# Gathered attention: unread identity products before every tile, scatters and later gathers spread out

## The reference

```python
# L2 feed-forward: one expert of seven per token, and a shared one
sel, p = the expert with the highest sigmoid, and its probability
switched = sum over e of where(sel == e, p, 0) * swiglu(x, ew1[e], ew2[e], ew3[e])
x = x + 0.5 / total_weight * swiglu(x, sw1, sw2, sw3) + switched / total_weight

# L3 attention: x normalised is the query, the context is key and value
logits = jnp.einsum('bsd,btd->bst', q, k) / jnp.sqrt(d_k)
logits = jnp.where(mask == 0, NEG, logits)
attn = jax.nn.softmax(logits, axis=-1)
o = jnp.einsum('bst,btd->bsd', attn, v)
x = x + layernorm(o) * gamma + beta
```

## Time and profile before

| | us |
|---|---|
| median of 3 runs | 2151.9 |
| lowest, highest | 2150.73, 2154.13 |
| the profiled execution | 2150.0 |
| its span | 2148.3 |
| TensorE busy | 1907.1 (89%) |
| VectorE busy | 1628.0 (76%) |
| ScalarE busy | 1364.7 (64%) |
| GpSimd busy | 1104.0 (51%) |
| L3a's gathers, first and last start | 1636.1, 1722.5 |
| L3a's transpositions of xhat, first and last start | 1661.8, 1785.4 |

### The profile page before, as it was taken

How to read it: one execution, slowest core, us unless ns; L and a number is a source line. 1 busy time by engine, 2 the same in 40 slices (tenths; PEclk the granted TensorE clock), 3 DMA queues, 4 the chain that set the end, 5 groups by cost and what they waited for, 6 DMA issues and landing times. The chain is left out here.

```text
span 2148.3 us, 86799 instructions
## 1 busy us (share of the span) xinstructions
PE 1907.1 (89%) x32111; PEld 1451.7 (68%) x32111; DVE 1628.0 (76%) x3712; ACT 1364.7 (64%) x3729; POOL 1104.0 (51%) x1286
## 2 busy tenths in 40 slices
PE   5999987989999979999989995999993973799998
PEld 3777754767777758888867773887772431677776
DVE  6788877866777768888856667777664786699998
ACT  4677766655555545666645554667772753599997
POOL 5566632873333325555568882756775754233332
PEclk9999996999999989999999997999996555799999
DMA  5111111000000002000001110113442520000000
GB/s 123 46 47 48 48 40 39 21 6 18 14 14 15 14 27 87 1 0 0 0 21 35 35 30 16 47 61 110 139 142 76 145 70 22 2 17 15 15 15 21
DMA packets 174358, 87.98 MB, mean 41 GB/s; under 512 B 70892, under 2 KB 168840, under 8 KB 174216
## 3 DMA queue, kind: packets, MB, share of 16 engines
q1 hardware_dynamic: 163656, 63.36, 11.0%
q0 software_dynamic: 7296, 21.38, 3.4%
q10 hardware_dynamic: 3264, 1.38, 0.3%
HBM read 66.13 MB, written 19.93 MB: 40 GB/s over the span
## 5 line engine op out<-in xcount | busy, mean ns | idle before, releaser
L1494 POOL TENSOR_TENSOR L1f_hl<-L1f_h,L1f_hh 128x512 fp32r<-128x512 f32 x128 | 167.2, 1307 | 126.1 <-DVE L1f_hh L1506 125.8
L1455 ACT ACTIVATE L1f_h<-L1f_H,L1f_w_b 128x512 f32<-128x512 f32 x192 | 132.0, 688 | 104.9 <-PE L1f_H L925 98.0
L399 POOL TENSOR_TENSOR L1a_wide<-L1a_flat,head_of_row 128x512 f32<-128x512 f32 x64 | 66.6, 1040 | 200.6 <-ACT L1a_flat L597 158.3
L399 POOL TENSOR_TENSOR L3f_wide<-L3f_flat,head_of_row 128x512 f32<-128x512 f32 x64 | 66.7, 1042 | 189.9 <-PE L3f_S L469 167.6
L1506 DVE CAST L1f_hh<-L1f_h 128x512 fp32r<-128x512 f32 x192 | 127.8, 672 | 31.7 <-ACT L1f_h L1455 30.6
L625 DVE TENSOR_REDUCE L1a_mx<-L1a_S 128x16 f32<-128x1024 f32 x64 | 78.4, 1224 | 80.8 <-PE L1a_S L469 80.8
L1841 ACT ACTIVATE L2f_both_act<-L2f_both_A 128x512 f32<-128x512 f32 x114 | 68.2, 598 | 92.1 <-PE L2f_both_G L925 91.2
L1872 DVE TENSOR_TENSOR L2f_both_h<-L2f_both_G,L2f_both_act 128x512 f32<-128x512 f32 x114 | 78.2, 686 | 63.6 <-ACT L2f_both_act L1841 63.1
L399 POOL TENSOR_TENSOR L0a_wide<-L0a_flat,head_of_row 128x512 f32<-128x512 f32 x64 | 66.6, 1040 | 95.0 <-ACT L0a_xhat L610 90.1
L625 DVE TENSOR_REDUCE L0a_mx<-L0a_S 128x16 f32<-128x1024 f32 x64 | 78.3, 1224 | 31.1 <-PE L0a_S L469 31.0
L1778 POOL TENSOR_TENSOR L2f_both_hl<-L2f_both_h,L2f_both_hh 128x512 fp32r<-128x512 f32 x66 | 85.6, 1297 | 31.4 <-ACT L2f_both_hh L1846 26.6
(11 more groups left out here) (534 smaller groups left out, 6815.6 us busy)
## 6 DMA issues: line engine op xcount, KB each, us to landing
L0a_mask_raw<-mask SPq DMA_DIRECT2D x256, 32.0 KB, 1.8
sorted_x<-L1f_zero SPq DMA_DIRECT2D x4, 1408.0 KB, 12.3
L2f_both_xhat<-sorted_x SPq DMA_DIRECT2D x22, 256.0 KB, 3.9
sorted_y<-L2f_both_y_out SPq DMA_DIRECT2D x22, 256.0 KB, 3.9
L0a_ctxT<-ctx_T SPq DMA_DIRECT2D x64, 64.0 KB, 1.9
L1a_ctxT<-ctx_T SPq DMA_DIRECT2D x64, 64.0 KB
L1a_mask_raw<-mask SPq DMA_DIRECT2D x256, 0.1 KB
L2a_ctxT<-ctx_T SPq DMA_DIRECT2D x64, 64.0 KB
```

Source lines behind the costliest of these rows:

```text
L399: pool.tensor_tensor(wide[:, s], flat[:, s, :].rearrange("p (b n) -> p b n", b=B2).unsqueeze(2).broadcast_to([P, B2, 4, S]), c.head_of_row ...
L1455: act.activation(h[:, q % 3, :], psH[:, q % 2, :], ACT.Relu, bias=b1[:, q:q + 1]).then_inc(h_kept, 1)
L1494: pool.tensor_tensor(hl[:, q % 3, :], h[:, q % 3, :], hh[:, q % 3, :], ALU.subtract).then_inc(hl_pool, 1)
```

## The change

Three edits in two functions.

1. `swiglu`: GpSimd issues 8 scatters at once. The other 56 follow in the shared part, four to a group of tiles: two behind the first pair of products of group u, one behind the second, one behind the third, for u from 0 to 13.
2. `gather_attention`: the first 20 gathers (`FREE`) are issued before the loop. Gather t from 20 on stands at step t-10 (`AHEAD = 10`) and waits for the transposition of tile t-22 (`xT_done`).
3. `gather_attention`: ahead of each tile's transposition, and ahead of its wait for `xhat`, TensorE multiplies a bf16 identity of 128x128 with itself into an unused part of the same PSUM bank, 48 times for tile 0 (behind a wait for the statistics of the first eight tiles), 8 times for tiles 1 to 15, 4 times from tile 16 on. Nobody reads these products.

```diff
 def swiglu(c, name, sems, r, IP, E):
 
+    EARLY = 8
...
-            for t in range(NT):
+            def scatter(t):
                 pool.indirect_dma_start(r.sorted_x, bass.IndirectOffsetOnAxis(ap=r.place[:, t:t + 1], axis=0),
                                         r.xhat[:, t, :], None).then_inc(scattered, 16)
 
+            for t in range(EARLY):
+                scatter(t)
+
             def step(i, r_):
                 for q in range(IC):
+                    for u, s in shared_at(i, r_, 2):
+                        first = EARLY + u * GT + (0, 2, 3)[q]
+                        for t in range(first, min(first + (2, 1, 1)[q], NT)):
+                            wait(pool, a_done, u * IC + q + 1)
+                            scatter(t)
...
-    LAST, AHEAD = 20, 24
+    LAST, AHEAD, FREE = 20, 10, 20
...
-                for i in range(-AHEAD, NT + 44):
-                    for t, q in at(i, -AHEAD):
+                for i in range(-FREE, NT + 44):
+                    early = range(i + FREE, i + FREE + 1) if i < 0 else ()
+                    late = range(i + AHEAD, i + AHEAD + 1) if FREE <= i + AHEAD < NT else ()
+                    for t in (*early, *late):
                         n = t // GR
                         if t % GR == 0 and n >= 2:
                             pool.wait_ge(gathered[n % 2], 16 * GR * (n // 2))
+                        if t >= FREE:
+                            pool.wait_ge(xT_done, max(t - FREE - 1, 1))
...
                     for u, s in at(i, 12):
+                        wait(pe, xT_kept, u - 1)
+                        if u == 0:
+                            pe.wait_ge(x_stats, GR)
+                        for _ in range(48 if u == 0 else 8 if u < 16 else 4):
+                            pe.matmul(psX[:, u % 2, P:2 * P], c.ident_bf[:, :], c.ident_bf[:, :], start=True,
+                                      stop=True, skip_group_check=True)
                         wait(pe, xhat_made, u + 1)
-                        wait(pe, xT_kept, u - 1)
                         pe.transpose(psX[:, u % 2, 0:P], xhat[:, s, :], c.ident[:, :]).then_inc(xT_done, 1)
```

## The result

| | us |
|---|---|
| before, median of 7 runs (lowest, highest) | 2151.66 (2149.88, 2154.64) |
| after, median of 7 runs (lowest, highest) | 2159.49 (2158.95, 2161.70) |
| ratio, with its 95% interval | 1.0036 [1.0027, 1.0046] |
| profiled execution of after, its span | 2161.49, 2159.8 |

The changed kernel is slower by 7.8 us. The forecast was 2149, "same", with 2160 as its upper end: the time lies just inside the range and the sign is wrong. The 1.3 us ahead of it are of that sort: from the first scatter to that transposition it takes 323.8 us before and 324.0 after.

A forecast was written before the change was run, and what follows sets the result against it. TensorE at half clock, then a GpSimd queue, VectorE and TensorE again bound the gathered attention. Scatter 0 and the last transposition at 1782.8 for 1785.4 make -2.6 from the median 2151.9: 2149 us, range 2138 to 2160.

The forecast's parts named there:

- What bounds the kernel now: Gathered attention: TensorE at half clock to 1715, a 12 us GpSimd queue, VectorE to 1769, then TensorE again.
- Scatter, term 0: Shared part: spreading the 64 scatters gains nothing; sorted rows' load at 1444; up to about 2 us if cover were gone.
- Gathers, gain 11.4 less 2.6: Gathered attention: first finished rows 11.4 us earlier with GpSimd never waiting, 2.6 given back by step 56, 8.8 left.
- Tile 22 at 1695.5: Gathered attention: tile 22's transposition at about 1695.5, taken as the place where the clock falls.
- Products: Before the transpositions: a tile with eight products takes 2.55 us at half clock, 1.35 at full; with four, 2.13 or 1.10.
- Clock: Gathered attention: full clock within the first few tiles, falling at tile 22 and not coming back; 2.13 us a tile after.
- The sum, -2.6: Whole kernel: last transposition at 1782.8 instead of 1785.4, the 38.0 us behind unchanged, so 2149 us.
- Rival 1: Gathered attention: full clock holds to the end and TensorE leaves the path; -12.2 us, 2139.7; chance 0.26.
- Rival 2: Gathered attention: the clock hardly rises, products cost TensorE time and late tiles delay gathers; +17.4 us, 2169.3; chance 0.17.
- Rival 3: Gathered attention: ten moved gathers block VectorE, step 56 on comes 9.5 us later; about 2155 us; chance 0.07.

The follow-up runs named there:

- e10_spread: The changed kernel without the gathers' waits for transpositions and without the unread products; 2144.73 us, ratio 0.9975 to the kernel before.
- e4_unpaced: The changed kernel without the wait of gathers 20 to 63 for a transposition; products and order stay; 2149.84 us, ratio 0.9990 to the kernel before.
- e12_late0: The changed kernel without the gathers' waits and without the four products of tiles 16 to 63; 2145.01 us, ratio 0.9975 to the kernel before.
- e14_eight: The changed kernel without the gathers' waits, with eight products instead of four at tiles 16 to 63; 2146.61 us, ratio 0.9973 to the kernel before.
- e15_ahead16: As e10_spread, but with AHEAD = 16 in place of 10; 2147.97 us, ratio 0.9982 to the kernel before.
- the distance 25: The changed kernel with gathers waiting for the transposition 25 tiles back instead of 22; 2173.15 us on that occasion, 2151.00 on another.

## Why the prediction was wrong

**What bounds the kernel now** held: TensorE at half clock in the first part, a queue on GpSimd in the middle, VectorE behind it. One reading there is off, and nothing rests on it: slices 32 to 34 begin at 1.66 ms and not at 1.72.

**Scatter, term 0:** right. Ratio 1.0001 alone; TensorE is at 10.00 of 10 and clock 1.00 from 1420 to 1430, and SP's first load of sorted rows starts at 1444.79, forecast 1444.

**Gathers, gain 11.4 less 2.6:** this is the step that failed, and in it one clause, "with GpSimd never waiting". For the order alone the working is good: 10.6 us at the finished rows (e10_spread), of which 3.4 are given back, so 7.2 are left at tile 63 for 8.8. But GpSimd does wait, 20 times and 22.7 us in all, and the end comes 10.2 us later where 2.6 less was forecast. I had both halves of the ring in the text, "gather t waits for tile t-22" and "VectorE waits at every eighth step for a whole group of gathers", and used each only in one direction: the first to ask whether TensorE makes gathers late, the second for holes in which the clock might fall. I never went once round and compared the distance, five steps of TensorE between the transposition of tile 8k-15 and that of 8k-10, with the time of a lap: from 1697.52 to 1708.42, 10.9 us here, 9.1 without the 1.8 of GpSimd catching up. Five steps are 8.5 us at 1.70 and 6.1 at the 1.215 us of a tile with four products at full clock. The faster TensorE would go, the more of it the ring takes back, and in the hole that this makes the clock fell (at 1704.9; TensorE had stood still since 1702.7).

**Tile 22 at 1695.5:** measured 1708.42, or 45.4 us after the first transposition where I had given it 33.7. With the products alone it needs 36.1, since the clock comes up for good later than I took it (tiles 6 to 10 at half); the gathers' new order makes that 37.7 (e4_unpaced), and the other 7.7 are the waits.

**Products:** prices a little high at half clock and a little low at full. A tile with eight products takes 2.48 us at half clock, with four 2.055 (forecast 2.55 and 2.13), and 1.44 and 1.215 at full (forecast 1.35 and 1.10): a tile by itself takes some 0.97 at full, and not half of 1.70. The 48 are one row:

```profile
1653.74 4.43 PE L2124 MATMUL L3a_X<-ident_bf 128*128 128x128 bf16 x48 [23.21 <-DVE L3a_x_stats L2206]
1663.06 0.48 PE L2127 MATMUL L3a_X<-ident,L3a_xhat 128*128 128x128 f32 x1 [4.89 <-ACT L3a_xhat L2151]
```

48 in 4.43 us is 0.092 each, since the clock rises at 1657.1, when three quarters of that time are over. It is back at half from 1660.5, before there is a tile to use it.

**Clock:** rise within the first few tiles and fall at tile 22, not to come back: as forecast in place, some 8 us late in time (1704.9, less the 1.3 of this execution, for 1695.5). The place is partly luck: it is where the ring makes its hole, and without the waits the clock fell at tile 27 (1709.2 in e4_unpaced). That the late tiles cost 2.055 and not 1.70 is in the forecast; the ends show 4.3 us for it (e4_unpaced less e12_late0).

**The sum, -2.6,** is what the changed kernel does without its waits: e4_unpaced has 2149.8, forecast 2149. This is partly luck. Tile 22 comes 4.0 us later there than I worked out, and from tile 22 to 63 it takes 83.1 us for 87.3.

**Rivals.** Rival 1 (clock holds, -12.2) did not come; and e14_eight, with 78 us at full clock in the three stretches above, speaks against its gain: taking TensorE off the path gives little where VectorE is full already. No run held the clock to the end, so its 3.4 us for the last nine tiles were not tested. Rival 2 has the mechanism nearest to the truth: gathers that come later than the queue in front of them would have let them, because TensorE's transpositions are late. It put this at a clock that hardly rises, from step 44 on, and the price at 17.4; it showed first at tile 22, with the gathers of tiles 32 to 39 and with the clock up, and cost 10.7 us at tile 63. Rival 3 (the moved gathers hurt VectorE) is not borne out. VectorE's steps 48 to 56 take 17.65 us in e10_spread with gathers beside them and 17.9 in e15_ahead16, where all but the last gather are through; the kernel before, also without a gather there, has 16.2, so the steps differ without gathers too, and by far less than the rival's 9.5. The instructions themselves settle it: in L3a of e10_spread VectorE's sum of 128x128 takes 0.342 us on average with a gather beside it (36 cases), 0.339 with nothing (6), and 1.01, at most 2.08, with one of GpSimd's 512-column instructions (13). The rule that I had set beside this rival, from the Trainium skill, "SBUF — State Buffer", section "Who interferes with whom", that writing descriptors and some VectorE instructions exclude each other at a shared port, leaves no mark of that size on these steps. In after the same steps take 20.1, in e4_unpaced 16.7. VectorE waits for only 0.5 us of the 20.1; what is longer is single instructions beside GpSimd's of 512 columns. The same line, held and free:

```profile
1740.22 1.78 DVE L1967 SCALAR_TENSOR_TENSOR L3a_x_tmp<-L3a_x_tmp 128x8 f32<-128x8 f32 x1
1740.69 1.28 POOL L2077 TENSOR_TENSOR x_all<-x_all,L3a_w_beta 128x512 f32<-128x512 f32 x1
...
1743.54 0.17 DVE L1967 SCALAR_TENSOR_TENSOR L3a_x_tmp<-L3a_x_tmp 128x8 f32<-128x8 f32 x1
```

Tiles 35 to 54 take 43.8 us in after and 39.8 in e4_unpaced: 4.0 of the 13.5 us that the waits cost are there, 9.6 lie ahead of tile 35. That the waits move GpSimd's long instructions beside more of VectorE's, and that this makes the 4.0, was read from the two traces and not tested by itself.

The part of the change that helps is the new order by itself. e10_spread, 2144.7 us, beats both kernels, by 0.25% and 0.7%; with the 48 and the eights (e12_late0) it is the same within the measurement.

## What to carry to other kernels

When a change makes an engine wait for one that waits for it, go once round the ring: count the steps of the loop between the event waited for and the instruction that is held up, and compare their time with the time of a lap, at the pace the change is meant to bring. A wait for a whole group counts from its last member. Ask of a faster clock what takes over as the bound before paying for it; and price parts in pairs as well as alone: here the parts made 2.4 us and the whole 10.2.

## What the hardware showed that I had not expected

- Full clock can be on while little is done: 6.7 us at 1.00 with TensorE busy for 2.43 of them, and 48 products whose clock was gone 2.6 us before the first tile.
- With eight products a tile the clock went up three times and down three times between tiles 6 and 63 (e14_eight), with hardly any cost: 2.7 us by the ends to e10_spread.
- In the changed kernel VectorE's instructions of 8 or 16 columns take up to 2.0 us beside GpSimd's of 512 columns, for 0.14 to 0.17 otherwise; its sums of 128 columns take 0.34 us with a gather beside them and without.
- An engine that only waits for itself can lose 2.4 us, and ScalarE 23.6 us, while GpSimd issues indirect transfers in a row, on one occasion and not on another of the same chip. The kernel before took 2251 us then, and the ones with spread scatters 2173 to 2204. On that occasion the distance 25 was ahead of no wait at all (2173.2 and 2180.2), which otherwise is the other way round (2151.0 and 2145.0), though these two differ in the late products too. A comparison of kernels that issue many such transfers should be looked at on more than one occasion.
